# Layer 0 of an interaction tower from four product tiles and a squares operand, with the last additions over d on GpSimd

## What is computed

```
x0 = xk = e                                       # [1024, 32 fields, 16]
for W in (W0, W1, W2):                            # [32, hk, 64]
    xk = relu(einsum('bmd,bhd,mhk->bkd', x0, xk, W))
    outs.append(sum(xk, axis=2))                  # sum over d
h = concatenate([*outs, dense_ctx], axis=1)       # 192 + 16
h = relu(h @ W_top1 + b_top1); h = relu(h @ W_top2 + b_top2)
y = h @ W_top3
```

## Time and profile before

| | us |
|---|---|
| median of three runs | 644.87 |
| lowest, highest | 644.58, 645.04 |
| the profiled execution | 644.13 |
| its span, first to last instruction | 642.3 |
| PE busy | 584.2 |
| DVE busy | 584.5 |
| POOL busy | 469.8 |
| ACT busy | 358.1 |

### The profile page before, as it was taken

The page is one execution under the profiler, slowest core; times in us unless marked ns, Lnnn a source line. Parts: engine busy times, 40 slices in busy tenths (PEclk is TensorE's granted clock), DMA queues, the critical chain, the costliest instruction groups (busy, mean ns, idle before and its releaser), DMA issues.

```text
span 642.3 us, 7779 instructions
## 1 busy us (share of the span) xinstructions
PE 584.2 (91%) x2896; PEld 209.1 (33%) x2896; DVE 584.5 (91%) x329; ACT 358.1 (56%) x594; POOL 469.8 (73%) x405
## 2 busy tenths in 40 slices
PE   0078999999998989999999999999999999999998
PEld 0023333232322323333334323333334323333455
DVE  1039899999999999999999999999999999999994
ACT  0006474657556465747676465747576565736552
POOL 6677769798888888888979788888979793803011
PEclk9999999999999999999999999999999999999999
DMA  5286596637181825547280826456370916300000
GB/s 162 46 320 155 220 289 166 264 65 298 35 284 50 259 106 153 212 80 285 53 310 5 278 85 195 170 119 245 64 300 15 299 53 202 160 3 2 1 2 1
DMA packets 27138, 96.51 MB, mean 150 GB/s; under 512 B 7414, under 2 KB 12540, under 8 KB 22876
## 3 DMA queue, kind: packets, MB, share of 16 engines
q1 hardware_dynamic: 18908, 93.90, 43.5%
q0 software_dynamic: 8192, 2.11, 2.7%
HBM read 80.25 MB, written 15.73 MB: 149 GB/s over the span
## 4 chain that ended last, share of the span: by engine, by line
DVE 42%; PE 27%; issue 12%; POOL 10%; DMA 5%; SPq 1%; ACT 1%; DVEq 0%; POOLq 0%; ACTq 0%
DVE prod L489 41%; PE acca L590 10%; PE accb L590 8%; POOL emb L362 7%; DMA rows<-field_dram 3%; PE acc L560 3%; POOL prod L380 3%; PE spread L633 2%; DMA field_dram<-zb_field 1%; PE accb L611 1%; PE acc L611 1%; SPq L280 1%; DVE prod L470 1%; DVE za L494 0%; ACT zb_field L720 0%
## 5 line engine op out<-in xcount | busy, mean ns | idle before, releaser
L362 POOL DMA_INDIRECT emb<-in_table,idx x256 | 247.2, 966 | 77.8 <-issue 67.6
L590 PE MATMUL acca<-prod,w 128*64 128x512 f32 x1024 | 229.1, 594 | 3.3 <-DVE prod L489 2.1
L590 PE MATMUL accb<-prod,w 128*64 128x512 f32 x960 | 216.4, 596 | 13.3 <-DVE prod L489 13.3
L380 POOL TENSOR_TENSOR prod<-rows,mates 128x1024 f32<-128x1024 f32 x70 | 164.4, 2380 | 16.0 <-issue 15.6
L489 DVE TENSOR_TENSOR prod<-rows,x1a 128x2048 f32<-128x2048 f32 x64 | 145.6, 2278 | 5.2 <-ACT x1a L725 2.5
L489 DVE TENSOR_TENSOR prod<-rows,x1b 128x2048 f32<-128x2048 f32 (+1 forms) x65 | 145.7, 2245 | 1.3 <-PE accb L590 0.7
L489 DVE TENSOR_TENSOR prod<-rows,x2a 128x2048 f32<-128x2048 f32 x64 | 145.7, 2277 | 1.1 <-PE accb L590 0.8
L489 DVE TENSOR_TENSOR prod<-rows,x2b 128x2048 f32<-128x2048 f32 x64 | 145.6, 2277 | 0.0
L590 PEld LDWEIGHTS acca<-prod,w 128*64 128x64 f32 x1024 | 71.7, 137 | 145.8 <-issue 136.1
L590 PEld LDWEIGHTS accb<-prod,w 128*64 128x64 f32 x960 | 65.6, 137 | 155.7 <-issue 113.7
L725 ACT ACTIVATE x1a<-acc 64x512 f32<-64x512 f32 x62 | 35.3, 570 | 124.5 <-PE acc L560 123.8
(11 more groups left out here) (74 smaller groups left out, 256.4 us busy)
## 6 DMA issues: line engine op xcount, KB each, us to landing
rows<-field_dram SPq DMA_DIRECT2D x30, 2048.0 KB, 13.6
field_dram<-zb_field SPq DMA_DIRECT2D x32, 256.0 KB
mates<-field_dram SPq DMA_DIRECT2D x16, 512.0 KB, 3.8
emb<-in_table,idx POOLq DMA_INDIRECT x256
field_dram<-zb_field SPq DMA_DIRECT2D x32, 128.0 KB
field_dram<-zb_field SPq DMA_DIRECT2D x16, 192.0 KB
rows<-field_dram SPq DMA_DIRECT2D x2, 1024.0 KB, 7.0
rows<-field_dram SPq DMA_DIRECT2D x1, 1536.0 KB, 12.6
```

The lines of the kernel that those rows point to most:

```text
L362: pool.indirect_dma_start(out=emb[q % EMBS][:, j * EMB:(j + 1) * EMB], out_offset=None, in_=table, in_offset=bass.IndirectOffsetOnAxis(ap= ...
L380: nc.gpsimd.tensor_tensor(prod0[:, (q * L0 + k) % RING0, :], rows[:, slot(q, t), :], mates[:, :], ALU.mult).then_inc(s_prod0p, 1)
L590: mm = nc.tensor.matmul(acc[j % 2][side * HID:(side + 1) * HID, :], (w1 if layer == 1 else w2)[:, step, :], prod[:, (made(layer, s, half, ...
```

## The change

Layer 0 uses four product tiles: tiles 1, 2 and 3 of `rows`, and a new one, `across`, whose partitions 32b to 32b+31 hold the fields at a shift of 4(b+1) rows from their mates. The shift differs by block of 32 partitions, so `across` comes in four transfers of 32 partitions. Squares are no product tile any more: the 32 fields come once more into a small tile `squares` [64, 512] (first half of the columns in partitions 0 to 31, second half in 32 to 63), ACT squares it in place, and PE contracts each half over 32 partitions. The product tiles have a buffer each in place of a ring. SP issues the four transfers of `across` behind `mates`, and the two of `squares` before the rows, after a wait for the layer-0 sums of the period before. The first period's rows come as tile 1, tiles 2-3, the squares' fields, tile 0, tiles 4-7.

GpSimd's `add_halves` gets a fourth addition, 2 to 1, with `za` or `zc` as its output; DVE keeps only the last reduction of the program. `h2` lies in a free part of `h1`.

```diff
-LAYER0_TILES = (0, 1, 2, 3, 4)
+LAYER0_TILES = (1, 2, 3)
+MATES, FIELDS_LISTED = 104, 32
+def across_of(q):
+    return field_of(MATES + q % FIELDS_LISTED + 4 * (q // FIELDS_LISTED + 1))
...
-    L0 = len(LAYER0_TILES)
-    RING0 = 5
+    L0 = len(LAYER0_TILES) + 1
+    RING0 = 4
-    FIRST = [(0, 2), (2, 2), (4, 1), (5, 3)]
+    FIRST = [(1, 1), (2, 2), (0, 1), (4, 4)]
...
-        SUM0[2 * q - 2, 1] = [(k, q) for k in range(3, L0)]
+        SUM0[2 * q - 2, 1] = [(SQUARES, q), (L0 - 1, q)]
...
             def mates_in(q):
                 sp.dma_start(mates[:, :], part).then_inc(s_mates, 16)
+                for b in range(BLOCKS):
+                    at = q % LISTS * LENGTH + MATES + 4 * (b + 1)
+                    part = bass.AP(field_dram.tensor, at * N, [[N, FIELDS], [1, N]])
+                    sp.dma_start(across[b * FIELDS:(b + 1) * FIELDS, :], part).then_inc(s_across, 16)
+            def fields_in(q):
+                wait_for(sp, s_l0, q * (L0 + 1))
+                for c in range(2):
+                    at = (q % LISTS * LENGTH + MATES) * N + c * HALF
+                    part = bass.AP(field_dram.tensor, at, [[N, FIELDS], [1, HALF]])
+                    sp.dma_start(squares[c * FIELDS:(c + 1) * FIELDS, :], part).then_inc(s_fields_in, 16)
...
             def product0(q, k):     # GpSimd
+                    pool.wait_ge(s_across, (q + 1) * BLOCKS * 16)
+                if k == 1:
+                    pool.wait_ge(s_rows[0], q * 16)
+                wait_for(pool, s_l0, summed_before(q - 1, k) + 1)
+                other = across[:, :] if k == 0 else rows[:, slot(q, LAYER0_TILES[k - 1]), :]
+                nc.gpsimd.tensor_tensor(prod0[:, k, :], other, mates[:, :], ALU.mult).then_inc(s_prod0p, 1)
...
-                nc.gpsimd.tensor_tensor(by_d[:, :, 0:PAIR], by_d[:, :, 0:PAIR], by_d[:, :, PAIR:QUAD], ALU.add).then_inc(done, 1)
+                nc.gpsimd.tensor_tensor(by_d[:, :, 0:PAIR], by_d[:, :, 0:PAIR], by_d[:, :, PAIR:QUAD], ALU.add).then_inc(s_pair, 1)
+                pool.wait_ge(s_pair, n)
+                nc.gpsimd.tensor_tensor(to, by_d[:, :, 0], by_d[:, :, 1], ALU.add).then_inc(done, 1)
...
             def layer0(k, q):       # TensorE
+                if k == SQUARES:
+                    pe.wait_ge(s_squares, q + 1)
+                    for c in range(2):
+                        part = slice(c * FIELDS, (c + 1) * FIELDS)
+                        mm = nc.tensor.matmul(acc0[c * HID:(c + 1) * HID, :], w0[part, SQUARES, :], squares[part, :],
+                                              start=False, stop=False)
+                    mm.then_inc(s_l0, 1)
+                    return
...
+            def square_fields(q):   # ScalarE
+                act.wait_ge(s_fields_in, (q + 1) * 2 * 16)
+                nc.scalar.activation(squares[:, :], squares[:, :], ACT.Square).then_inc(s_squares, 1)
```

## The result

| | before | changed |
|---|---|---|
| median, us | 644.79 | 648.38 |
| lowest, highest | 644.58, 645.04 | 647.32, 649.52 |
| the profiled execution | 644.13 | 647.32 |
| its span | 642.3 | 645.4 |

The ratio is 1.0055 (95% interval 1.0043 to 1.0068), 3.6 us longer. The forecast was 641.3 and its range ended at 648.0; the sign is wrong as well. A second comparison, with new profiles of both kernels on one chip, gave a slower kernel too: 647.18 us against 644.94, ratio 1.0035 (1.0021 to 1.0048). Runs of the changed kernel spread more than those of the kernel before (646.35 to 649.52 against 644.47 to 645.51); what the runs show of the reason stands further down.

What follows compares the result with a forecast made beforehand. DVE bounds the middle, with PE 0.32 us behind. Reductions -3.7, POOL -1.0, changes of shape +1.2, start -0.1 make -3.6 us: 641.3 from 644.87. Range 639.3 to 648.

Steps and rivals of the forecast that it cites:

- SP and the transfers: Start, periods 0 to 2: six more issues and 640 KB more per period; 0.1 us gained, between 1.3 gained and 2.3 lost.
- Rival 3: Start: small transfers are slow and arrivals of periods 0 to 2 lose 2.3 us more, 643.6 us; chance 0.10.
- the first product later than 49.6: Sign for slow small transfers at the start: the first 128x2048 product on DVE starts later than 49.6 us.
- Reductions: DVE between 118 and 548 us: 19 reductions removed at 0.195 us each, 3.7 us gained.
- POOL's two waits: DVE's waits of 0.78 us before 186.02 and 0.2 one period earlier go, as POOL has fewer products: 1.0 us gained.
- Changes of shape: PE, around the squares: changing matmul shape in and out costs 0.3 us in four periods without slack, 1.2 us lost.
- d: PE's cost per period for changing shape into and out of the squares: 0.2 to 0.45 us, taken as 0.3.
- Rival 1: PE: the two squares' halves don't run side by side, d becomes 1.16, sum +8.2 us, 653.1 us; chance 0.18.
- Rival 2: PE: changes of shape cost more than the slack, d about 0.6, sum +0.4 us, 645.3 us; chance 0.12.
- Later periods: Middle of the program: rows come some 4 us later, hidden because they are used 25 us or more after issue.
- The ACT square: ACT, between input2(j,0) and input1(j+2,0): 0.57 us each, 9 us in all, hidden by ACT's 6.99 us of idle time.
- POOL's fourth addition: POOL, in place of DVE's reductions: between 0.2 and 0.4 us, 24 times, say 7 us.

Runs made afterwards that it cites:

- two single-period kernels: Kernel before plus the change's six small transfers behind mates, in period 0 alone, then in period 1 alone: 648.75 and 648.15 us against 644.99.
- the three with the extra transfers: Kernel before plus the change's six small transfers, in periods 0 and 1 (652.81 us against 644.94), period 0 alone (648.75), period 1 alone (648.15 against 644.99).
- e11_five_tiles_first: Changed kernel with periods 0 and 1 as before (five product tiles, no across, no squares): 640.86 us against 644.99 for the kernel before, ratio 0.9934.

## Why the prediction was wrong

**The step that failed is "SP and the transfers"**, the start's term of the sum. It was -0.1 us, with bounds of -1.3 and +2.3; it was +7.2 (+6.7 in the second comparison, 121.33 against 114.67 on one chip). All else in the sum held, so with the right term the same working gives a slower kernel. Four things went into the miss, and the bounds held none of them in full:

- *Issue time.* The list of ends was made from bytes and rates alone. That the four issues of across hold up the rows by 1.84 us (37.34 for the second rows transfer in place of 35.50), and six of them those of period 1 by 2.8, was never added, although the prediction names the issues. The products of the last two tiles start 46.38 - 43.62 = 2.8 us later; the bound was 1.8. Rival 3 and its sign, "the first product later than 49.6", pointed here, with a third of the price.
- *The squares on the path.* PE contracts them between tiles 2 and 3 (48.67 to 49.68), at a place where it waits for nothing else. The last product ends at 48.74 and its contraction starts 0.9 us later. DVE ends its products 1.6 us later than before (48.74 and 47.11), and 1.6 + 0.9 make the 2.5 us by which the first product of 128x2048 is late. The forecast counted the squares against the slack of steady steps and forgot the one stretch where layer 0 is awaited.
- *The delay carried on.* Each period's arrival was reckoned against the kernel before, as if period 0 had cost nothing. Its 2.5 us reach ACT's queue, thence the fields of period 1, the list and the rows: 65.02 against 59.69, and the products end at 78.4 where 73.9 to 75.9 was given. The two single-period kernels show that such delays add (5.1 + 3.2 for 8.5).
- *The clock.* No row of before shows it below full, and I took PE's speed as given. In layer 0 of period 0 PE waits for at most 1.56 us at a time in the kernel before; with late rows it is 1.6 to 5.5 us, and in both profiles of the changed kernel above, as in the three with the extra transfers, the clock fell during or shortly after a wait of PE in layer 0 of period 0 or 1 (1.85 to 5.5 us). Its price in the first profile: the transpose starts 83.01 - 74.89 = 8.1 us after DVE starts the products of tiles 1 to 3, where in the second profile, with the clock full there, it is 83.00 - 77.57 = 5.4. That is 2.7 us, and 0.4 more in the transpose. These are read off two profiles; no run changes the clock alone, so its share of the loss is not shown by an experiment.

How the 7.2 us come about isn't the same in each execution. In the first profile DVE ends period 1's products at 78.4, 3.3 us later than before (75.04), and the other 3.9 come behind that, where DVE waits for PE. In the second it ends them at 81.1, since the clock had fallen in period 0 already. That is 5.4 us later than in the kernel before on the same chip (75.65), and 1.2 more follow. Both are at 121.2 to 121.3 in step 3.

**What held.**

- *Reductions*: 3.7 us forecast, 3.67 measured by putting them back.
- *POOL's two waits*: gone, 1.0 us. What the forecast had only as an aside, that POOL needs the lighter product load to take the additions, is a matter of 5.3 us (a rest of 529.8 where 528.2 less 3.7 was expected).
- *Changes of shape*: d = 0.30, costing 1.0 us behind step 3's second product and 0.27 just ahead of it (1.2 forecast with period 2 counted). From that product to the end the three measured terms give -3.7 - 1.0 + 1.0 = -3.7, and the measurement is -4.1. The last 0.4 lies behind DVE's last operation (3.0 us to the end before, 2.65 now) and was in no term.
- *Rival 1*, with 0.18 the likeliest way to a slower kernel, did not happen; the kernel is slower by another road. Rival 2 neither.
- *Later periods*: rows some 4 us later and hidden. `e11_five_tiles_first` shows that for periods 2 to 15 together.
- *The ACT square* takes 0.61 to 0.63 us (0.57 forecast) and POOL's fourth addition 0.30, between its bounds.

## What to carry to other kernels

Price the first periods as their own program. Their transfers, issues and small instructions can be on the path where the steady state hides them, and a delay in the first period is handed to the second and adds to its own. Where a change is bought with more transfers and pays back only in the steady state, let it begin in the first period that has the cover. And if an engine will wait longer than it did before, ask what else its speed depends on; to find out which part of a program a difference stands in, look for one instruction behind which all kernels run alike, and compare on both sides of it.

## What the runs showed of the hardware

- *The granted clock fell during or shortly after PE's waits, but not with each.* In the changed kernel it fell 1.1 us after the end of a wait of 1.85 us (ahead of 76.17, first profile) and 1.4 us after one of 2.32 us (ahead of 43.05, second profile), while waits of 2.15 us (ahead of 47.66, first) and 2.16 us (ahead of 78.85, second) left it full. What decides between them these runs don't show, nor that it makes the spread of 646.35 to 649.52. In the four runs of the result the longer ones have the lower mean clock (0.995 at 647.32, 0.992 at 647.91, 0.989 at 648.84 and 649.52), in those of the second comparison they don't (0.992 at 647.36, 0.995 at 646.35 and 648.63).
- *Four transfers over 32 partitions against one over 128*: 512 KB each way, and the tiles behind them are 1.9 us later, 1.4 of it issue (2.5 to 2.7 later against the kernels of the same chip).
- *Two matmul halves over 32 rows each, into one bank*, run side by side: four instructions in 1.0 us with both changes of shape, where four of 128 rows take 0.86.
- *Left open*: on two chips the kernels took 7 to 8 us longer, the kernel before 653.0 and 653.2 us. In the changed kernel's profile there PE ended its contractions for period 1 at 82.0, and ACT's eviction that waited for them started at 92.15; the trace puts the wait down to no engine of the core, and the DMA engines were 6 to 10% busy meanwhile. The rests are those of the other chips, so such waits lie ahead of step 3's second product, and I did not find their cause.
